# A two-layer local-attention block: the last steps of the layers issued from a written-out list

## The reference, cut to what matters

```python
x = layernorm(x + causal_attention(x))            # one head of 64, over the whole sequence
y = x
for l in range(2):                                # the layers
    h = shift_token(y)                            # second half of the columns comes from the row above
    q, k, v = split(h @ wqkv[l])                  # 8 heads of 64
    q, k = rotary_xpos(l2norm(q) * qs[l], l2norm(k) * ks[l])
    y = y + local_attention(q, k, v) @ wo[l]      # windows of 128 rows: own window and the one before
    h = shift_token(y)
    h = normalise(h) * ln_g[l] + ln_b[l]
    a, g = split(h @ w1[l] + b1[l])               # twice 682 columns
    y = y + (a * gelu(g)) @ w2[l] + b2[l]
return layernorm(x + y)
```

## Time and profile before

| | |
|---|---|
| median of 3 runs | 2774.15 us (2766.67 to 2779.47) |
| the profiled execution | 2765.12 us |
| its span, first to last instruction | 2762.9 us |
| PE, DVE, ACT, POOL busy | 97%, 82%, 68%, 60% of the span |
| granted PE clock, mean | 0.983 |

### The profile page before, as it was taken

The page is one execution under the profiler, slowest core; times in us unless marked ns, Lnnn a source line. Parts: engine busy times, 40 slices in busy tenths (PEclk is TensorE's granted clock), DMA queues, the critical chain, the costliest instruction groups (busy, mean ns, idle before and its releaser), DMA issues.

```text
span 2762.9 us, 65920 instructions
## 1 busy us (share of the span) xinstructions
PE 2674.0 (97%) x22240; PEld 2347.6 (85%) x22240; DVE 2257.7 (82%) x7122; ACT 1889.5 (68%) x4798; POOL 1649.6 (60%) x1753
## 2 busy tenths in 40 slices
PE   8998699999999999999999999999999999999996
PEld 5776478888888888888988888888888888888886
DVE  5776578888888888888887888888888888988884
ACT  5565367767777777777776777767777767777773
POOL 3444456666656566655555666676666666666662
PEclk9999799999999999999999999999999999999998
DMA  5566210000000000000002311110111110011110
GB/s 181 182 198 196 101 44 28 24 28 25 24 26 28 26 26 28 21 26 28 26 26 81 107 35 32 36 36 27 32 35 32 36 35 29 30 35 32 36 30 22
DMA packets 144511, 140.39 MB, mean 51 GB/s; under 512 B 16024, under 2 KB 126128, under 8 KB 143408
## 3 DMA queue, kind: packets, MB, share of 16 engines
q1 hardware_dynamic: 144176, 136.18, 15.6%
HBM read 80.02 MB, written 51.92 MB: 48 GB/s over the span
## 4 chain that ended last, share of the span: by engine, by line
PE 83%; DVE 2%; DMA 1%; ACT 1%; issue 1%; SPq 1%; POOL 0%; DVEq 0%; POOLq 0%; ACTq 0%
PE p_wide L95 13%; PE p_wide L97 12%; PE p_wide L96 12%; PE p_values L1680 9%; PE p_turn L1668 8%; PE p_mixed L95 5%; PE p_mixed L97 5%; PE p_mixed L96 5%; PE p_score L95 4%; PE p_turn L1635 2%; PE p_score L96 2%; PE p_score L97 2%; PE p_turn L1642 2%; PE p_mixed L1600 1%; PE p_mixed L1698 1%
## 5 line engine op out<-in xcount | busy, mean ns | idle before, releaser
L1114 POOL TENSOR_TENSOR prob<-prob,rinv 128x512 f32<-128x512 f32 (+1 forms) x512 | 498.4, 989 | 504.6 <-DVE rinv L1402 504.2
L1217 ACT ACTIVATE prob<-prob,least 128x256 f32<-128x256 f32 (+1 forms) x1024 | 498.5, 488 | 68.4 <-DVE least L1394 65.4
L1394 DVE CUSTOM_DVE_ANT_0 prob<-p_score,mask,inv_norm 128x256 f32<-128x256 f32 (+1 forms) x1024 | 442.1, 459 | 53.3 <-issue 50.0
L1092 POOL TENSOR_TENSOR inv_norm<-norm_clipped,minus_half 128x8 f32<-128x8 f32 x256 | 439.0, 1715 | 74.2 <-DVE norm_clipped L1360 67.4
L1226 ACT ACTIVATE pT<-p_turn 128x512 f32<-128x512 f32 (+1 forms) x512 | 270.4, 566 | 245.5 <-PE p_turn L1668 243.8
L95 PE MATMUL p_wide<-hT_h,w_h 128*128 128x256 f32 (+1 forms) x1408 | 414.1, 294 | 5.3 <-DVE hT_l L1450 4.2
L97 PE MATMUL p_wide<-hT_h,w_l 128*128 128x256 f32 (+1 forms) x1408 | 396.5, 282 | 0.0
L96 PE MATMUL p_wide<-hT_l,w_h 128*128 128x256 f32 (+1 forms) x1408 | 395.8, 281 | 0.0
L95 PE MATMUL p_wide<-wqkv_h,xT_h 128*128 128x512 f32 x768 | 330.0, 430 | 6.2 <-DVE rope_sin L1344 4.0
L1248 ACT ACTIVATE gelu<-p_wide,columns 128x256 f32<-128x256 f32 x320 | 151.7, 474 | 228.5 <-PE p_wide L97 226.9
L97 PE MATMUL p_wide<-wqkv_h,xT_l 128*128 128x512 f32 x768 | 307.2, 400 | 0.0
(11 more groups left out here) (134 smaller groups left out, 7620.7 us busy)
## 6 DMA issues: line engine op xcount, KB each, us to landing
x_tile<-x_rows SPq DMA_DIRECT2D x192, 128.0 KB, 2.1
a_wraw<-in_w_all SPq DMA_DIRECT2D x32, 264.0 KB, 4.4
w_high<-a_wraw_h SPq DMA_DIRECT2D x32, 264.0 KB, 2.4
w_low<-a_wraw_l SPq DMA_DIRECT2D x32, 264.0 KB, 3.0
a_x<-in_x SPq DMA_DIRECT2D x32, 256.0 KB, 4.7
x_rows<-a_x SPq DMA_DIRECT2D x64, 128.0 KB, 1.8
x_tile<-x_rows SPq DMA_DIRECT2D x128, 64.0 KB, 2.0
mid_rows<-x_mid SPq DMA_DIRECT2D x128, 64.0 KB, 1.5
```

The lines of the kernel that those rows point to most:

```text
L1092: pool.tensor_tensor(r[:, t.slot(2), heads], rt[:, heads], half[:, heads], ALU.pow).then_inc(pool_r[n], 1)
L1114: pool.tensor_tensor(p, p, rinv[:, 2 * m:2 * m + 2].unsqueeze(2).to_broadcast([P, 2, cols.stop - cols.start]), ALU.mult).then_inc(pool_p, 1)
L1217: act.activation(prob[:, h, cols], prob[:, h, cols], ACT.Exp, bias=least[:, h:h + 1], scale=-1.0, accum_out=rsum[:, h:h + 1]).then_inc(act ...
L1394: dve.tensor_tensor_reduce(prob[:, h, cols], p_score[h % 2][:, c0 + cols.start:c0 + cols.stop], mask[:, a.slot(2), cols], r[:, a.slot(2), ...
```

## The change

1. The steps are run as before up to a point: 61 of them on PE and ACT, 60 on DVE, POOL and SP. All later calls stand in a function `last_steps` of each engine, tile by tile, in an order of their own. They are the same calls: 248 on PE, 291 on ACT, 507 on DVE, 142 on POOL. Tiles 116 to 127 pass through most of their work there.
2. On PE the waits are taken out of the functions and out of `vacant`, and written ahead of each call as `after(...)`; waits that an earlier one implies are left out. In `step` the calls and their order are the same.
3. The write to `took` is gone from `least_of`.
4. `middle` in layer 1 waits for the residual's first part (`pool_r1`), not for the residual with x1 added (`pool_res`).
5. The two table loads of the rotation signal two semaphores, and tiles are numbered 0 to 127 throughout; addresses are the same.

In ACT's new list the calls change from `exponential` to `gelu` or back 26 times; in the old order the same calls change 12 times. In PE's new list the calls go into or out of a run of `values` or of `scores` 97 times, in the old order 74 times.

```diff
-    for w in range(0, TAIL + 2, 2):
-        step(Step(DEPTH * B, w))
+def all_steps(step, first, end):
+    for n in range(first, end):
+        step(Step(n))
...
# DVE
                         need(dve, pe_pT, a.done(4, 2 * group - 2))
-                        at = 2 * a.slot(2) + group
-                        dve.memset(took[:, at:at + 1], 0.0)
...
-                    need(dve, pool_res, c.done(1, -1))
+                    if c.g < LAYER + 2:
+                        need(dve, pool_res, c.done(1, -1))
+                    else:
+                        dve.wait_ge(pool_r1, c.done(1, -1 - LAYER))
...
# PE, step: one of the calls
-                if T(5):
-                    vacant((act_pT, T(6), 4, 4), (act_pT, T(6), 4, 2), (dve_kT, T(5), 1, 1), ...)
+                if T(5):
+                    after((act_pT, T(6), 4, 4))
+                    after((pool_p, T(5), 4, 2))
                 turn_probs(T(5), 1)
...
# ACT, last_steps: a stretch of it
+                gated_high(Q(114), 2)
+                k_high(T(119))
+                gated_high(Q(114), 3)
+                exponential(T(118), 5)
+                gelu(Q(114), 4)
+                gelu(Q(114), 5)
+                exponential(T(118), 6)
+                exponential(T(118), 7)
...
# PE, last_steps: the same stretch
+                widen(Q(114), 4)
+                values(T(118), 0)
+                widen(Q(114), 5)
+                scores(T(119), 0)
+                turn_x(T(121))
+                turn_probs(T(118), 1)
+                project_q(T(120))
+                project_v(T(120))
+                scores(T(119), 1)
+                turn_probs(T(118), 2)
...
# PE, last_steps: its end
+                widen(Q(124), 0)
+                after((dve_gt, Q(122), HF + 1, 6))
+                widen(Q(124), 1)
+                after((dve_oT, T(127), 1, 1))
+                output(T(127))
+                after((dve_gt, Q(124), HF + 1, 1))
+                widen(Q(124), 2)
...
+                widen(Q(124), 5)
+                after((dve_hn, T(127), 1, 1))
+                turn_h(Q(126))
+                after((dve_hv, Q(126), 1, 1))
+                narrow(T(124))
+                after((dve_hT, Q(126), 1, 1))
+                widen(Q(126), 0)
+                after((dve_gt, Q(124), HF + 1, 6))
+                widen(Q(126), 1)
+                after((dve_x, T(124), 1, 1))
+                narrow(T(125))
+                after((dve_gt, Q(126), HF + 1, 1))
+                widen(Q(126), 2)
...
+                widen(Q(126), 5)
+                after((dve_gT, Q(126), HF + 1, 6))
+                narrow(T(126))
+                after((dve_x, T(126), 1, 1))
+                narrow(T(127))
...
# DVE, last_steps: near its end
+                middle(T(127))
+                gated_low(Q(124), 0)
+                gated_low(Q(124), 1)
+                gated(Q(124), 2)
+                gated_low(Q(124), 2)
+                gated(Q(124), 3)
+                statistics(T(127))
+                gated_low(Q(124), 3)
+                gated(Q(124), 4)
+                gated(Q(124), 5)
+                normed(T(127))
+                gated_low(Q(124), 4)
+                gated_low(Q(124), 5)
+                h_affine(Q(126))
+                h_low(Q(126))
...
-            all_steps(pe, step)
+            all_steps(step, 0, 61)
+            last_steps()
```

More of the change, by code:

```diff
@@ L766, in _, with __init__ @@
             all_batches(step)
+TILES = DEPTH * B * NW
+LAYER = B * NW
 class Tile:
[L772 to L775, removed]
+    def __init__(self, g):
+        self.g, self.layer, self.batch, self.window = g, g // LAYER, g // NW, g % NW
         self.first = self.window == 0
     def done(self, per, more=0):
-        return per * NW * self.i + per * self.off + more
+        return per * self.g + more
@@ L782, in slot, with back, __init__ @@
     def slot(self, ring):
-        return self.off % ring
+        return self.g % ring
     def uses(self, ring, more=0):
-        return NW // ring * self.i + self.off // ring + more
-    def is_number(self, n):
-        return isinstance(self.i, int) and NW * self.i + self.off == n
+        return self.g // ring + more
+    def back(self, n):
+        return Tile(self.g - n)
 class Pair:
-    def __init__(self, i, off, layer):
-        self.i, self.off, self.layer = i, off, layer
-        self.first, self.second = Tile(i, off, layer), Tile(i, off + 1, layer)
+    def __init__(self, first):
+        self.first, self.second, self.layer = first, first.back(-1), first.layer
@@ L800, in done, with __init__ @@
     def done(self, per, more=0):
[L802 to L807, removed]
+        return per * (self.first.g // 2) + more
 class Step:
-    def __init__(self, i, w, layer=None):
-        self.i, self.w, self.layer = i, w, layer
+    def __init__(self, n):
+        self.n = n
     def tile(self, lag):
[L818 to L822, removed]
+        g = 2 * self.n - lag
+        return Tile(g) if 0 <= g < TILES else None
@@ L824, in pair @@
     def pair(self, lag):
         first = self.tile(2 * lag)
[L827 to L835, removed]
-    for w in range(0, TAIL + 2, 2):
-        step(Step(DEPTH * B, w))
+        return Pair(first) if first else None
+def all_steps(step, first, end):
+    for n in range(first, end):
+        step(Step(n))
 def layers_phase(nc, x_d, mid_d, wh_d, wl_d, tab_d, out, shared):
@@ L895, in layers_phase @@
         w_in = {n: sem(f"w_{n}_in") for n in ("k", "q", "v", "wo", "w1", "w2")}
-        tab_in = sem("tab_in")
+        tab_in = [sem(f"tab_in{n}") for n in range(2)]
         x_in = [sem(f"x_in{n}") for n in range(4)]
@@ L1072, in _ @@
+            all_steps(step, 0, 60)
+            last_steps()
             for n in range(2):
@@ L1580, in _, with after @@
+            all_steps(step, 0, 60)
+            last_steps()
         @block.tensor
         def _(pe):
-            def vacant(*readers):
-                for semaphore, last_reader, per, more in readers:
-                    if last_reader:
-                        pe.wait_ge(semaphore, last_reader.done(per, more))
+            def after(*done):
+                for semaphore, tile, per, more in done:
+                    if tile:
+                        pe.wait_ge(semaphore, tile.done(per, more))
@@ L1587, in vacant @@
                         return
             def arrived(name, tile):
-                if tile.is_number(LAYER) or tile.is_number(0) and name not in ("q", "k", "v"):
+                if tile.g == LAYER or tile.g == 0 and name not in ("q", "k", "v"):
                     times = tile.layer + (name not in ("q", "k", "v"))
@@ L1826, in step @@
+                    if not T(7):
+                        after((dve_xT, T(2), 1, 1))
                 turn_x(T(1))
```

1675 lines of the change are left out of this document (1602 added, 73 removed).

## The result

The changed kernel takes 2781.39 us (median of 6 runs, 2781.26 to 2784.06), the kernel before beside it 2771.53 us (6 runs, 2761.67 to 2779.47). The ratio is 1.0042, 95% interval [1.0026, 1.0059]; forecast were 2770 us, 3.8 us less than before. In a later comparison (e8) the ratio of the same two kernels was 1.0026 [1.0009, 1.0043].

A forecast was written before the change was run, and what follows sets the result against it. PE's instruction stream bounds the kernel, save gaps at the end. Gain 7.4 less 1.3 (table loads) and 2.3 (seams) gives 3.8 us off the median 2774.15: 2770 us, range 2757 to 2783, the forecast's own 2764 to 2775.

The forecast's parts named there:

- Waits and `took` elsewhere: Outside the tail's order: PE's rewritten waits, dropped `took` writes and weaker `middle` wait change 0 us, other end 2 us.
- the waits or `took` mattered: Sign in the full steps: they still take 150.0 us per four, PE full, clock 1.00; otherwise these mattered.
- More seams on PE: Ahead of `output(127)`: 23 more changes to or from `scores` or `values`, 0.1 us each, cost 2.3 us; ends 1 and 3.
- More table loads on ACT: Ahead of `output(127)`: 14 more loads of 1.283 us; idle 6.5 us plus clock 1.7, 8.2 for 6.9, cost 1.3 us.
- The walk: From `widen(114,4)` to `turn_probs(118,2)`: ACT late behind two loads, PE waits 2.2 us; about 2 again before `turn_probs(122,2)`.
- Rival 2: Ahead of `output(127)`: all 14 loads reach PE, 18.0 us, whole 12.8 us slower, 2787 us; chance 0.12.
- The end: Behind `output(127)`: the new order fills gaps, loss falls from 16.9 to 9.5 us, gain 7.4; ends 4 and 9.
- One stretch at the half clock: Behind `output(127)`: the clock falls once in place of twice, losing 3.0 us.
- Rival 3: Behind `output(127)`: the new order does not remove the gaps, the end gives only 4 us, total 2774; chance 0.14.
- PE's waits written anew: On PE throughout: the rewritten waits cost 0 us, since PE's queue is ahead of its array.
- Forecast for the tail: From PE's call 248 from the end to the last matmul: 236.8 us where before it took 240.6.
- slower: Whole kernel over 2788 us, beyond what a measurement can tell: half of rival 2 and a rest unseen, chance 0.09.

The follow-up runs named there:

- e8: Changed kernel as it is, timed once more beside the kernel before: 2779.13 us, ratio 1.0026, four full steps 150.26 us, tail 245.06 us.
- e5: Kernel before without the 256 writes to `took`, its tile still allocated in place: 2773.61 us, ratio 1.0007, four full steps 150.01 us.
- e4: Kernel before without the writes to `took` and without its tile: 2774.34 us, ratio 1.0026 to before, four full steps 150.27 us.
- e7: Changed kernel with the tile `took` allocated where the kernel before has it, never written: 2777.15 us, ratio 1.0006 to before, tail 244.94 us.
- e14: Kernel before with two `values` calls moved in every step, four more changes into or out of `values`: 2818.82 us, ratio 1.0172.
- e12: Changed kernel with the tile `took`, Identity for Gelu in the tail so ACT loads no table there: 2770.95 us, ratio 0.9997 to before.
- e11: Kernel before, its tile, waits and order kept, with only the new list's end: 2762.94 us, ratio 0.9963, tail 234.52 us.
- e2: Changed kernel with its steps run to the end in the old order, new waits kept: 2774.82 us, ratio 1.0031 to before.
- e3: As e2, but with PE's old waits as well: 2778.15 us, ratio 1.0028 to before, four full steps 150.27 us.

## Why the prediction was wrong

**The step that failed: "Waits and `took` elsewhere", "I take 0, and as the other end 2 us".** The argument was about DVE: it has idle time, PE doesn't wait for it, so 256 writes less change nothing. That is right (e5: 150.00 us without the writes). The part that counts was the line with the tile. It was left out of the forecast, and of the description of the change, which names the writes alone and says that addresses are the same; those of the tiles in SBUF are not. Over the layers it cost 4.0 us by the two profiles, 4.4 by the means of six and six, and 0.26 us on each of some 16 groups of four steps, 4.2 us, by the table above; e4 measured 1.0026, 6.6 us, with an interval from 1.4 to 13.0. The prediction's own sign did show it: full steps other than 150.0 mean that "the waits or `took` mattered". It left only instructions to look for as the reason.

**"More seams on PE", 2.3 us: mis-sized.** Beyond idle time and clock, the new list takes 7.3 us more than before (8.0 in e7 less 0.7). Sorted by the calls on which it lies, with the same calls in full steps of layer 1 as the measure, it is: 3.6 us on `values` and the calls beside them, 1.3 us on those beside `scores`, 2.9 us on the calls directly ahead of one of PE's waits (3.5 us on 23 such calls in e7, 0.6 on 3 in before), and -0.4 us on all others. The first two are the seams, 4.9 us in place of 2.3: a change costs 0.155 us and not 0.1 (e14), which makes 3.6 us of 23; the other 1.3 stay open. Changes that touch neither `values` nor `scores` aren't the reason: up to `output(127)` a call of one name is followed by a call of another, both of them neither, 99 times in the new list and 108 in the old. The 2.9 us belong to the waits. The idle time in brackets starts where the record of the last matmul ends, 0.28 us after its start for 256 columns, where in a run the next starts after 0.12 us; so a wait costs more than its bracket.

**"More table loads on ACT", 1.3 us: mis-sized.** The 14 loads came, 11 to 25 in the tail, 1.283 us each. PE idle ahead of `output(127)` 9.0 us (forecast 6.5, before 5.2), in e7 9.5. With the clock, 9.0 + 0 in the changed kernel and 9.5 + 1.7 in e7 against 6.9: 2.1 to 4.3 us in place of 1.3, and 5.0 to 7.2 with the 2.9 us just named. The price of all 25 loads in the new order is 4.2 to 5.9 us (e12). The walk had the right place and chain, `normalise(122)` behind two loads, but its 2 us became four waits with 3.8: ACT is late with the copy for the next `values`, and DVE, which waits 1.25 us for the same exponentials, with the `rope_sin` ahead of `project_v`. Not all of it is the loads': without them (e12) both waits on `prob` are gone, but `values(122,2)` waits 1.55 us and `project_v(124)` 0.84. Rival 2 named the mechanism, with 18.0 us for 14 loads; all 25 cost a third of that at most.

**The end, 7.4 us: right.** 7.0 measured in the two profiles, with waits of 1.58, 1.09, 2.40 and 0.52 against 1.9, 1.6, 2.5 and 0.5 (of the first, the forecast's own terms, 6.7 less 5.0, give 1.7). "One stretch at the half clock" were two, 10.0 us together; before had 13.7. Rival 3 is out: 5.2 us came even without the new list (e11, 33.8 and 1.36 against 40.4).

**PE's waits written anew: 0, right.** e2 and e3 differ by nothing beyond the scatter, 150.29 and 150.27. The weaker wait of `middle` is in both.

**The whole.** Forecast for the tail 236.8, measured 243.6: the end gave 7.0 us, and the part ahead lost 10.1 where the forecast had 3.6. The tail of the old order itself isn't one number: nine profiles have 240.5 to 243.4, with 10.2 to 20.5 us at the half clock at the end; the new list has 241.7 to 245.1 in four. On means the new list loses 10.7 us up to `output(127)` and gains 8.8 behind it, about 2 us of loss in sum. With 4.2 to 6.6 of the place that makes 6 to 9 us. The medians are 9.9 and 7.5 us apart, and by the intervals of the two ratios the difference is 7 to 16 and 2 to 12 us: the sum fits, but the intervals are too wide to test it closely. That a chance of 0.09 was given to "slower" was too little for a reason that lay outside the list of steps: nothing in it moved a tile, so nothing priced it.

## What to carry to other kernels

In a kernel whose one engine is full, compare its pace first, window against window with the same instructions: when that moves with no wait, look at what lies where, and keep every tile's address when a small one is dropped, or leave padding in its place. Price a change between kinds of matmul from the calls on both sides of it and not from the gap, and try the end of a schedule by itself: here it held all the gain of the tail, and the reordering ahead of it all the cost. Take a wait's price from the starts of the calls on both sides of it, too: the bracketed idle time leaves part of it out.

## What the runs showed of the hardware that was not expected

- The place of the tiles in SBUF changes the pace of a full PE: four steps took 149.25 to 150.29 us over six placements, with the same instructions, clock 1.00 and no wait. Single calls moved more: `widen` 1335 to 1370 ns, `output` 1487 to 1516, `narrow` 2053 to 2130. The Trainium skill ("SBUF — State Buffer", section "Operand start alignment") tells where an operand may start, and says that its runs "timed nothing"; all placements here start at multiples of 32 bytes, and still differ.
- Going into a call of `values` and out of it again costs 0.31 us: 0.08 us in the gap ahead of it, 0.12 on its eight matmuls and 0.11 on the first matmul of the projection behind them (e14).
- The row of the loads in the changed tail, ACT's groups by line:

```profile
L1441 ACT ACT_TABLE_LOAD x13 | 16.7, 1283 | 0.2
L1410 ACT ACT_TABLE_LOAD x12 | 15.4, 1283 | 0.2
```

Thirteen and twelve loads with 0.2 us of idle time in all ahead of each group, where the earlier trace rows has 0.1 for six and for five. In the timeline above a gelu starts 1.29 us after its load started and 0.01 after it ended, and the load for the exponentials 0.49 us after the last gelu began. The Trainium skill ("ScalarE: Activation LUTs", section "What ACT_TABLE_LOAD costs") adds a drain of about 1380 ns to each; no run here shows one. An estimate by its 2.66 us: 25 loads would hold ACT for 66.5 us of the tail; by the rows it is 32.1.
